# Transposing x tiles 4 to 7 by DMA on SP's queue instead of on TensorE and ScalarE

## The reference, cut to what matters

```python
def fake_quant(x, scale, zp):
    q = jnp.clip(jnp.round(x / s + z), 0, 255)
    return (q - z) * s
# layer 1
x = x + matmul(fake_quant(layernorm(x)), fake_quant(ctx))
# layer 2, on y = layernorm(x)
result = einsum('bsd,od->bso', y, base_w) + base_b
w_full = softmax of the two largest of (y @ gate_w.T), zero elsewhere
x = x + result + 2.0 * (lora_B applied to w_full * (y @ lora_A.T))
```

## Time and profile before

| | |
|---|---|
| median of 3 runs | 180.59 us |
| profiled execution, its time | 179.92 us |
| its span, first to last instruction | 178.0 us |
| TensorE clock granted, mean | 0.981 |
| PE / PEld / DVE / ACT / POOL busy | 94% / 70% / 69% / 43% / 9% |
| SP's DMA queue (q1) | 22.06 MB, 33.3% of 16 engines' span |
| GpSimd's DMA queue (q0) | 7.34 MB, 21.9% |

### The profile page before, as it was taken

How to read it: one execution, slowest core, us unless ns; L and a number is a source line. 1 busy time by engine, 2 the same in 40 slices (tenths; PEclk the granted TensorE clock), 3 DMA queues, 4 the chain that set the end, 5 groups by cost and what they waited for, 6 DMA issues and landing times.

```text
span 178.0 us, 2466 instructions
## 1 busy us (share of the span) xinstructions
PE 167.0 (94%) x862; PEld 124.1 (70%) x862; DVE 123.3 (69%) x314; ACT 77.3 (43%) x132; POOL 16.2 (9%) x33
## 2 busy tenths in 40 slices
PE   5818999899999999999999999999999999999992
PEld 1314454479888888886788668876888688888881
DVE  0789948999999999799968834866856268411233
ACT  2269977995236096557432631339131101140100
POOL 3021204110010000000050101021010000100000
PEclk9995899999999999999999999999999999999999
DMA  5999999999993019803099426059118020420033
GB/s 108 395 420 411 367 412 348 272 256 217 414 345 59 0 64 295 351 2 120 32 220 205 89 47 118 0 96 198 63 17 221 4 93 25 76 41 4 0 118 118
DMA packets 9515, 29.55 MB, mean 166 GB/s; under 512 B 1184, under 2 KB 1184, under 8 KB 9504
## 3 DMA queue, kind: packets, MB, share of 16 engines
q1 hardware_dynamic: 7344, 22.06, 33.3%
q0 software_dynamic: 2016, 7.34, 21.9%
q10 hardware_dynamic: 144, 0.00, 0.0%
HBM read 22.05 MB, written 4.19 MB: 147 GB/s over the span
## 4 chain that ended last, share of the span: by engine, by line
PE 86%; DVE 9%; DMA 2%; issue 1%; ACT 1%; DVEq 0%; ACTq 0%
PE ps_even L929 25%; PE ps_odd L929 25%; PE ps_att L875 12%; PE ps_g L911 6%; PE ps_t L859 4%; PE ps_even L883 3%; PE ps_g L914 2%; DMA q_in<-in_scales 2%; DVE x_sb L617 2%; PE ps_t L850 2%; DVE stats L559 1%; PE ps_odd L972 1%; PE ps_even L972 1%; PE ps_even L971 1%; PE ps_odd L971 1%; PE ps_odd L970 1%
## 5 line engine op out<-in xcount | busy, mean ns | idle before, releaser
L929 PE MATMUL ps_even<-w_hi,yt 128*128 128x512 f32 x128 | 37.7, 397 | 0.0
L929 PE MATMUL ps_odd<-w_hi,yt 128*128 128x512 f32 x128 | 36.7, 403 | 0.0
L875 PE MATMUL ps_att<-c,c1t 128*128 128x512 f16 x96 | 25.7, 391 | 1.8 <-DVE c L606 1.8
L929 PEld LDWEIGHTS ps_odd<-w_hi,yt 128*128 128x128 f32 x128 | 23.5, 188 | 5.0
L929 PEld LDWEIGHTS ps_even<-w_hi,yt 128*128 128x128 f32 x128 | 23.5, 188 | 4.9
L929 PE MATMUL ps_even<-w_lo,yt 128*128 128x512 f32 x64 | 20.1, 391 | 0.0
L929 PE MATMUL ps_odd<-w_lo,yt 128*128 128x512 f32 x64 | 19.3, 393 | 0.0
L875 PEld LDWEIGHTS ps_att<-c,c1t 128*128 128x128 f16 x96 | 8.9, 100 | 11.6 <-issue 2.7
L351 ACT ACTIVATE ln_v<-mv,eps 128x1 f32<-128x1 f32 x16 | 4.7, 292 | 28.5 <-DVE mv L564 28.5
L911 PE MATMUL ps_g<-ag,yt 128*128 128x272 f32 x64 | 16.8, 336 | 0.0
L642 DVE TENSOR_TENSOR yt<-ps_t,yt 128x512 fp32r<-128x512 f32 x15 | 10.3, 685 | 9.2 <-ACT yt L420 9.0
(11 more groups left out here) (99 smaller groups left out, 259.7 us busy)
## 6 DMA issues: line engine op xcount, KB each, us to landing
ring<-in_ctx SPq DMA_DIRECT2D x12, 512.0 KB, 8.4
w_raw<-in_w_t SPq DMA_DIRECT2D x8, 512.0 KB, 9.5
x_sb<-in_base_b POOLq DMA_DIRECT2D x8, 512.0 KB, 5.9
out_x<-x_sb SPq DMA_DIRECT2D x16, 256.0 KB, 2.0
x_sb<-in_x SPq DMA_DIRECT2D x7, 512.0 KB, 6.2
x_sb<-zfix POOLq DMA_DIRECT2D x6, 512.0 KB, 6.3
x_sb<-in_ctx SPq DMA_DIRECT2D x4, 512.0 KB, 7.8
ag_raw<-in_ag_t SPq DMA_DIRECT2D x1, 544.0 KB, 6.6
```

The lines of the kernel that those rows point to most:

```text
L875: ins = pe.matmul(att_bank(t)[h][:, :], c1t[:, t % 4, k, :], c2[:, k, h * HALF:(h + 1) * HALF], start=(k == 0), stop=(k == CT - 1))
L929: pe.matmul(ffn_bank[t % 2][h][:, :], rows_of(part, t, k), w[:, k, h * HALF:(h + 1) * HALF], start=start, stop=False)
```

## The change

For tiles 4 to 7 TensorE's `transpose_c1` and ScalarE's `take_c1t` are gone. SP issues one DMA with `transpose=True` per tile, from `c1` (128x1024 f16) to `c1t`, on the queue of the loads and stores. It waits for `cut_x(t)` and for the attention of tile t - 4, which was the last reader of that slot of `c1t`. `attention(t, 0)` waits for the DMA's own semaphore. Since nothing subtracts 128 on the way any more, `cut_x` of these tiles takes the minimum with 255 and subtracts 128 in one instruction (Relu has removed the negative values), and `zero_point_row` adds nothing. On SP's list the DMA of tile 4 stands behind `load_context(15)`, that of tile 5 behind `store(1, 1)`, that of tile 6 behind `store(2, 1)`, that of tile 7 behind `store(3, 1)`. The order of all other work is as before.

```diff
--- before.py
+++ after.py
@@ -158,6 +158,7 @@
         c1_ready = sem("c1_ready")
         c1t_psum = sem("c1t_psum")
         c1t_ready = sem("c1t_ready")
+        c1t_in = {t: sem(f"c1t_in{t}") for t in range(TPB, TILES)}
         rowsum_ready = sem("rowsum_ready")
         rowfix_ready = sem("rowfix_ready")
         cact_ready = sem("cact_ready")
@@ -238,6 +239,11 @@
                     context_scaled(sp, k - RING)
                 sp.dma_start(context_raw(k), ctx_d[k]).then_inc(ring_in[k % RING], 16)
 
+            def transpose_c1(t):
+                sp.wait_ge(c1_ready, t + 1)
+                sp.wait_ge(att_done, t - 3)
+                sp.dma_start(c1t[:, t % 4], c1[:, t % 4, :], transpose=True).then_inc(c1t_in[t], 16)
+
             def load_ag():
                 sp.dma_start(ag_raw[:, :], ag_t).then_inc(ag_in, 16)
 
@@ -280,12 +286,16 @@
             load_x(7)
             for k in range(13, 16):
                 load_context(k)
+            transpose_c1(4)
             store(1, 0)
             store(1, 1)
+            transpose_c1(5)
             store(2, 0)
             store(2, 1)
+            transpose_c1(6)
             store(3, 0)
             store(3, 1)
+            transpose_c1(7)
             store(4, 0)
             store(4, 1)
             store(5, 0)
@@ -371,15 +381,13 @@
 
             def take_c1t(t):
                 act.wait_ge(c1t_psum, t + 1)
-                if t >= 4:
-                    act.wait_ge(att_done, t - 3)
-                act.activation(c1t[:, t % 4].rearrange("p k m -> p (k m)"), ps_th, ACT.Copy,
+                act.activation(c1t[:, t].rearrange("p k m -> p (k m)"), ps_th, ACT.Copy,
                                bias=-CENTRE).then_inc(c1t_ready, 1)
 
             def zero_point_row(t):
                 act.wait_ge(c1_ready, t + 1)
-                act.activation(junk[:, :], c1[:, t % 4, :], ACT.Copy, bias=-CENTRE,
-                               accum_out=rowsum[:, t:t + 1]).then_inc(rowsum_ready, 1)
+                act.activation(junk[:, :], c1[:, t % 4, :], ACT.Copy,
+                               bias=-CENTRE if t < TPB else 0.0, accum_out=rowsum[:, t:t + 1]).then_inc(rowsum_ready, 1)
                 if t == 0:
                     act.wait_ge(ss_ready, 1)
                 act.wait_ge(rowsum_ready, t + 1)
@@ -482,7 +490,6 @@
             split_y_hi(2, 1)
             scale_x(4)
             first_guess(1, 3)
-            take_c1t(4)
             split_y_hi(3, 0)
             exp_gate(2)
             for k in range(12, 15):
@@ -496,14 +503,12 @@
             exp_gate(3)
             first_guess(1, 4)
             zero_point_row(3)
-            take_c1t(5)
             first_guess(0, 6)
             split_y_hi(4, 0)
             split_y_hi(4, 1)
             scale_x(6)
             first_guess(0, 7)
             split_low_hi(3)
-            take_c1t(6)
             first_guess(1, 5)
             scale_x(7)
             exp_gate(4)
@@ -514,7 +519,6 @@
             split_low_hi(4)
             split_y_hi(5, 1)
             first_guess(1, 6)
-            take_c1t(7)
             exp_gate(5)
             split_y_hi(6, 0)
             split_y_hi(6, 1)
@@ -593,10 +597,15 @@
 
             def cut_x(t):
                 dve.wait_ge(qx_ready[t], 1)
-                if t >= 4:
+                if t >= TPB:
+
                     dve.wait_ge(c1t_psum, t - 3)
                     dve.wait_ge(rowsum_ready, t - 3)
-                dve.tensor_scalar(c1[:, t % 4, :], qx[:, t % 2, :], 0.0, QMAX, ALU.max, ALU.min).then_inc(c1_ready, 1)
+                    dve.tensor_scalar(c1[:, t % 4, :], qx[:, t % 2, :], QMAX, -CENTRE,
+                                      ALU.min, ALU.add).then_inc(c1_ready, 1)
+                else:
+                    dve.tensor_scalar(c1[:, t % 4, :], qx[:, t % 2, :], 0.0, QMAX,
+                                      ALU.max, ALU.min).then_inc(c1_ready, 1)
 
             def cut_context(k):
                 context_scaled(dve, k)
@@ -864,7 +873,10 @@
             def attention(t, k):
                 pe.wait_ge(c2_ready, CT * (t // TPB) + k + 1)
                 if k == 0:
-                    pe.wait_ge(c1t_ready, t + 1)
+                    if t < TPB:
+                        pe.wait_ge(c1t_ready, t + 1)
+                    else:
+                        pe.wait_ge(c1t_in[t], 16)
                     if t == 2:
                         pe.wait_ge(zfix_ready, 2)
                     if t == 3:
@@ -1045,7 +1057,6 @@
             transpose_low(1)
             for k in range(2, 5):
                 base(2, k)
-            transpose_c1(4)
             low_and_gate(2)
             lora(1, 0)
             lora(1, 1)
@@ -1069,7 +1080,6 @@
             low_and_gate(3)
             for k in range(0, 7):
                 base(3, k)
-            transpose_c1(5)
             base(3, 7)
             attention(5, 0)
             transpose_y(4, 0)
@@ -1080,7 +1090,6 @@
                 base(4, k)
             transpose_low(3)
             attention(5, 7)
-            transpose_c1(6)
             base(4, 4)
             base(4, 5)
             low_and_gate(4)
@@ -1100,7 +1109,6 @@
             transpose_y(5, 1)
             for k in range(0, 3):
                 base(5, k)
-            transpose_c1(7)
             base(5, 3)
             low_and_gate(5)
             attention(7, 0)
```

## The result

The changed kernel took 186.4 us (median of 4 runs, 183.7 to 187.5) beside 180.8 for the kernel before in the same measurement. It is slower. The profiled execution took 183.69 us, span 181.9, against 179.92 and 178.0 before: 3.9 us more in the span.

What follows compares the result with a forecast made beforehand. TensorE was taken to bound the kernel (86% of the span). Transposes removed, -1.84 us, plus a 0.65 wait at tile 4 make -1.19: 180.59 becomes 179.4 us, range 178.6 to 188.0, leaving out rivals 3 and 4.

Steps and rivals of the forecast that it cites:

- rival 2: Narrow writes make tile 4's wait exceed the gain: 181.5 us at a 4.1 us transfer, 184.6 to 186.7 at 6; chance 0.28.
- rival 3: Eight blocks transposed in turn, 11.9 us per tile, waits at tiles 4 to 7: about 198 to 201 us; chance 0.17.
- The saving: On TensorE, tiles 4 to 7: removing 4 x 8 transposes saves 1.84 us, all on the path, nothing else late.
- SP: SP's queue: four DMA issues of 0.53 us each; only stores stand behind them, and nobody waits for those.
- The transfer: One tile's DMA transpose: taken as 2.0 us of the DMA engines, near ends 0.70 and 4.1.
- rivals 3 and 4: Blocks in turn, 198 to 201 us, chance 0.17; value by value, 66 us each, over 400 us, chance 0.03.
- Tile 4: Tile 4's attention: DMA queued behind loads to about 75.2, landing at 77.65, so TensorE waits 0.65 us.
- A: Theory of the experiments: a transpose steps over all 16 DMA engines together, stalling while another queue's packet holds any one.
- Tile 5: Tile 5's attention: transpose shares engines with GpSimd's additions at half rate, lands about 99.8 at latest, before 100.36: no wait.
- The clock: TensorE's clock: put only in rival 3, where long waits lower it, some 2.2 us of work lost.
- Tiles 6 and 7: Attention of tiles 6 and 7: DMA room of 9.9 and 8.9 us, so no wait; tile 7 at most 0.2 late.
- The share of 1.09: DMA engines' share from 96 to 98 us before the change, read as full with GpSimd's additions, then nearly idle.

Runs made afterwards that it cites:

- e4: The kernel before, with tiles 6 and 7 alone transposed by DMA: 179.2 us, ratio 0.994 to the kernel before.
- e6: Changed kernel, GpSimd's additions held at tile 5 until its transpose landed, tile 4's first attention piece moved behind base(2, 5) and base(2, 6): 178.4 us, 0.989.
- e7: As e6, with GpSimd's additions also held at tiles 6 and 7 until the transpose has landed: 178.1 us, 0.987.
- e1: Changed kernel, GpSimd issuing the bias of tile 3 and zfix of tile 5 only after tile 5's transpose landed: 179.2 us, 0.995.
- e11: The changed kernel measured again, nothing altered, on the chip of the experiments: 184.0 us, ratio 1.021.
- e3: The kernel before, with tile 4 alone transposed by DMA: ratio 0.998 to the kernel before.
- e5: e1's kernel, with ScalarE issuing four plain 512 KB loads from HBM when tile 5's integers are ready: 180.9 us, 1.004.
- e8: Changed kernel with 12 filler matmuls on constants ahead of tile 5's attention, while TensorE waits: 183.2 us, 1.017.
- e9: e1's kernel, with ScalarE issuing ten small loads of 2 rows of 16 KB when tile 5's integers are ready: ratio 1.026.
- e12: e1's kernel, with ScalarE issuing one HBM-to-HBM copy of 2 x 128 KB when tile 5's integers are ready: 179.1 us beside 179.8, one run.

## Why the prediction was wrong

The forecast was 179.4 us, faster; it is 2% slower. The sum said -1.2 us and the span grew by 3.9. The 5.1 between them are the wait at tile 5 (2.5, put at nothing), the low clock after it (1.7, put at nothing), tile 4 (0.8 more) and the slower first pairs (0.3), less the 0.3 that are not accounted for. The chances stood closer to it than the forecast, 0.46 for slower and 0.42 for faster, but for other reasons: rival 2's 184.6 us is near the measured times by waits of 4.65 and 1.2, where 1.49 and 2.54 were seen, and that tile 5 landed near rival 3's 11.9 us is chance, for alone it lands after 3.1.

- *The saving.* Right: 1.84 us on the path, nothing else late in its place. e4, e6 and e7 have it. `cut_x` is 0.43 us as before.
- *SP.* Right that nobody waits for the stores behind the transposes. The issue is 1.24 to 1.85 us, not 0.53. At tile 4 it ends at 73.9, while the loads ahead still hold the engines, so it cost little there.
- *The transfer.* I took 2.0 us of the engines; alone it is 1.4. The bounds held (0.70 and 4.1), and rivals 3 and 4, blocks in turn and value by value, are out: 256-byte packets, 3.1 us for eight blocks. The Trainium skill (Advanced Engine Details and Errata, X-Bar Transpose (TRN2)) has it that such a DMA is as fast as a regular one: nearer than my rivals, but twice too good here, 1.4 us against 0.70 for the plain copy. The 1309 ns of the Trainium skill for one block (VectorE: DVE Perf Modes, The three transpose paths) do not multiply: eight land in 3.1 us.
- *Tile 4.* Right in place, twice as large: a wait of 1.49 for my 0.65, 1.3 in e1 and e11, but 0.4 in e3, e5 and e8. The landing comes between 77.4 and 78.6 in these, whether the issue was at 72.3 or 73.2, so what is on the engines before it sets it, and there my "from about 75.2" nearly holds: 80 of its 1,024 data packets started before 75.0. In the trace of the changed kernel packets of the transpose nearly stop from 76.1 to 77.3, just after one engine took a 16 KB packet of instructions (1.0 us, from 75.6). That fits A, but no run took the fetch away, so it is argued only.
- *Tile 5.* **The step that failed**: "At half rate until 98.2 it has done 3 us of work; even 4.1 lands at about 99.8, before 100.36." It landed at 103.8. I let the transpose share each DMA engine with GpSimd's additions as two ordinary queues do. The runs show another thing: with GpSimd on a quarter of the engines' time its packets took 0.31 us each instead of 0.02, and in e9 it nearly stopped for 1.2 us beside two packets of another queue. So the engines did not each share for themselves. While it waits it holds up what is behind it (e12) and beside it, so the additions are late too (zfix 11.9 us for 7.7), and at the worst both queues together moved 72 GB/s where one moved 217. e1 removes the additions and the landing is 3.4.
- *The clock.* I priced it in rival 3, for waits of 10 us, at 2.2 us of work. It was 1.7 after a wait of 2.5 (e8 shows it by its absence). After the 1.3 to 1.5 us at tile 4 the granted clock stayed at 1.00.
- *Tiles 6 and 7.* Right: no wait, landings 5.6 and 5.8 against 9.9 and 8.9 of room.

The share of 1.09 that I read from 96 to 98 was the sign. I took it for a queue to share; here the transpose came nearly to a stop beside it.

## What to carry to other kernels

Give a DMA transpose a stretch in which no other queue moves data, or hold those queues until it has landed: here the same transfer took 3.1 us alone, 5.6 to 7.4 beside one addition, 9.7 beside four plain loads and 11 to 16 beside several additions. With such a stretch at tile 5 the change gained 0.5% (e1), and with the wait at tile 4 gone too 1.1 to 1.3% (e6, e7). Read the room for it against that worst case, queue by queue, not against its bytes. And a wait of TensorE can cost more than its length: here 2.5 us brought 1.7 more, in work at half the clock, where 1.5 us brought nothing of the kind.

## What the runs showed of the hardware

- The DMA share says engines are held, not that they move data: 1.22 with 72 GB/s (98 to 100 us of the changed kernel), and 0.00 with 0 GB/s while two engines copied and 14 stood still (95 to 97 us of e12), since a packet counts where it starts.
- The transpose was 1,024 packets of 256 bytes; alone 1.4 us for 256 KB, some 190 GB/s, 3.1 us from issue to landing. One packet took 0.02 us alone (e7) and 0.31 with GpSimd's queue on 24.5% of the engines' time (98.5 to 100.5 us of the changed kernel).
- With two engines busy on a 64 KB copy and owing some 16 pieces of the transpose each, 16 packets of the stores behind it stood for 2.7 to 5.6 us instead of 0.08 (e12).
- An issue of it kept SP's queue 1.24 us at least (tile 6) and up to 2.8 (tile 6 of e12); what lengthens it was not isolated. A plain DMA's is 0.53.
- TensorE idle for 2.5 us was granted 0.50 of its clock soon after, and with 2.6 us of filler and 1.4 of idle time in the same place it kept 1.00.
